# A per-role adapter with layernorm on one Trainium2 core: where the role list is loaded, who spreads it, and the order of TensorE's first work

## The reference

```python
def _L0_cond_ref(role, hidden_states, W_down, b_down, W_up, b_up, gamma, beta):
    h = jnp.einsum('bsh,bhk->bsk', hidden_states, W_down[role]) + b_down[role][:, None, :]
    h = jax.nn.gelu(h, approximate=False)
    u = jnp.einsum('bsk,bkh->bsh', h, W_up[role]) + b_up[role][:, None, :]
    y = hidden_states + u
    mean = jnp.mean(y, axis=-1, keepdims=True)
    var = jnp.mean(jnp.square(y - mean), axis=-1, keepdims=True)
    yn = (y - mean) * jax.lax.rsqrt(var + LN_EPS)
    return yn * gamma[role][:, None, :] + beta[role][:, None, :]
```

## Time and profile before

| | us |
|---|---|
| median of 3 runs | 1421.34 |
| lowest and highest | 1421.17, 1422.79 |
| the profiled execution, its own time | 1421.44 |
| its span in the profile | 1419.7 |
| PE busy | 1405.4 (99%) |
| DVE busy | 1205.7 (85%) |
| ACT busy | 776.7 (55%) |
| POOL busy | 206.7 (15%) |

### The profile page before, as it was taken

The page is one execution under the profiler, slowest core; times in us unless marked ns, Lnnn a source line. Parts: engine busy times, 40 slices in busy tenths (PEclk is TensorE's granted clock), DMA queues, the critical chain, the costliest instruction groups (busy, mean ns, idle before and its releaser), DMA issues.

```text
span 1419.7 us, 29422 instructions
## 1 busy us (share of the span) xinstructions
PE 1405.4 (99%) x6194; PEld 1162.6 (82%) x6195; DVE 1205.7 (85%) x1462; ACT 776.7 (55%) x2048; POOL 206.7 (15%) x310
## 2 busy tenths in 40 slices
PE   8999999999999999999999999999999999999997
PEld 6888888888888888888888888888888888888886
DVE  7798988888888888888899888888888888888887
ACT  5555555555555555555555555555555555555554
POOL 5276311100000000000477310000000000000000
PEclk9999999999999999999999999999999999999999
DMA  7588777766666666666778766776665666566564
GB/s 227 164 234 233 217 202 213 203 200 199 192 185 195 200 189 185 200 199 185 215 228 246 210 204 195 193 221 194 197 195 183 196 200 189 185 195 202 186 188 147
DMA packets 209127, 283.62 MB, mean 200 GB/s; under 512 B 25894, under 2 KB 155814, under 8 KB 209104
## 3 DMA queue, kind: packets, MB, share of 16 engines
q1 hardware_dynamic: 201448, 269.40, 61.3%
q0 software_dynamic: 5984, 12.11, 4.9%
q10 hardware_dynamic: 1672, 1.86, 0.4%
HBM read 183.39 MB, written 99.88 MB: 200 GB/s over the span
## 4 chain that ended last, share of the span: by engine, by line
PE 96%; DVE 1%; issue 1%; DMA 1%; ACTq 0%; DVEq 0%; ACT 0%
PE p_up L1161 16%; PE p_up L1163 16%; PE p_up L1162 16%; PE p_down L1163 16%; PE p_down L1162 16%; PE p_down L1161 16%; DMA row<-in_L_cond_W_down 0%; DMA w_raw<-in_itok_B 0%; ACTq L275 0%; DVE row L909 0%; PE p_down L1204 0%; PE p_down L1209 0%; DVE row L884 0%; PE p_down L1215 0%; DVE row L931 0%
## 5 line engine op out<-in xcount | busy, mean ns | idle before, releaser
L1161 PE MATMUL p_up<-wu_hi,hT_hi 128*128 x1008 | 392.4, 389 | 0.3 <-DVE hT_lo L870 0.3
L1163 PE MATMUL p_up<-wu_hi,hT_lo 128*128 x1008 | 392.2, 389 | 0.0
L1162 PE MATMUL p_up<-wu_lo,hT_hi 128*128 x1008 | 392.1, 389 | 0.0
L1163 PE MATMUL p_down<-wd_hi,xT_lo 128*128 x1000 | 389.0, 389 | 0.0
L1161 PE MATMUL p_down<-wd_hi,xT_hi 128*128 x1000 | 389.0, 389 | 0.0
L1162 PE MATMUL p_down<-wd_lo,xT_hi 128*128 x1000 | 389.0, 389 | 0.0
L643 ACT ACTIVATE hT_hi<-p_hT 128x512 fp32r<-128x512 f32 x126 | 75.5, 599 | 383.0 <-DVE p_hT L864 380.5
L884 DVE SCALAR_TENSOR_TENSOR row<-p_up,row 128x1024 f32<-128x1024 f32 x126 | 154.2, 1223 | 126.1 <-PE p_up L1163 126.0
L623 ACT ACTIVATE xT_hi<-xT_raw 128x1024 fp32r<-128x1024 f32 x125 | 132.7, 1062 | 185.5 <-PE p_down L1163 184.0
L1161 PEld LDWEIGHTS p_up<-wu_hi,hT_hi 128*128 128x128 f32 x1008 | 189.1, 188 | 39.9 <-issue 0.7
L1163 PEld LDWEIGHTS p_up<-wu_hi,hT_lo 128*128 128x128 f32 x1008 | 189.3, 188 | 39.3
(11 more groups left out here) (192 smaller groups left out, 1008.5 us busy)
## 6 DMA issues: line engine op xcount, KB each, us to landing
x_quad<-in_x SPq DMA_DIRECT2D x508, 128.0 KB, 3.4
row<-in_x SPq DMA_DIRECT2D x126, 512.0 KB, 4.1
out<-row SPq DMA_DIRECT2D x126, 512.0 KB, 2.7
h_dram<-h SPq DMA_DIRECT2D x125, 256.0 KB, 4.1
h_quad<-h_dram SPq DMA_DIRECT2D x498, 64.0 KB, 1.9
w_raw<-in_L_cond_W_down POOLq DMA_DIRECT2D x64, 64.0 KB, 3.2
w_raw<-in_L_cond_W_up POOLq DMA_DIRECT2D x64, 64.0 KB, 3.6
row<-in_L_cond_W_up SPq DMA_DIRECT2D x16, 128.0 KB, 5.3
```

The costliest lines, as they stand in the source:

```text
L1161: pe.matmul(dst, a_hi, w_hi, start=first, stop=False)
L1162: pe.matmul(dst, a_hi, w_lo, start=False, stop=False)
L1163: return pe.matmul(dst, a_lo, w_hi, start=False, stop=last)
```

## The change

- The list of roles goes to one partition. The sort keys are made in that partition alone, in other scratch (`key` moves to `w_raw[1]`).
- PE spreads the first role to all partitions with a matmul against a row of ones (`ones_row`, made by POOL with one more memset) after 5 fillers; 21 fillers follow. DVE's `pick_rows` waits for it and copies it out of PSUM first.
- The three spreads of beta and b_down stand ahead of the first matmul of batch 0, and those of b_up a little earlier. ACT's copies wait for the new counts.
- PE loads the slots behind batch 0, whose weights are now at the fixed address 0, and then, ahead of batch 1, spreads the keys with two small matmuls: the row of keys to all partitions, and each key to its own partition. `sort_all` reads both from PSUM, and POOL waits for `key_spread` before it reuses `w_raw`.

```diff
-            sp.dma_start(role_row, role.partition_broadcast(P)).then_inc(roles_loaded, 16)
+            sp.dma_start(role_row, role.rearrange("(o b) -> o b", o=1)).then_inc(roles_loaded, 16)
...
+            pool.memset(ones_row, 1.0).then_inc(iotas_ready, 1)
...
-            pool.wait_ge(half_down, 1)
+            pool.wait_ge(key_spread, 1)
...
-            copy_param(2, p_up[1][:, :], BETA, H, beta_loaded)
+            copy_param(1, p_up[1][:, :], BETA, H, beta_loaded)
...
-            copy_param(1, p_hT[:, :], BD, K, bias_loaded)
+            copy_param(2, p_hT[:, :], BD, K, bias_loaded)
...
             def pick_rows():
-                chain(dve.tensor_scalar(pick_at[:, :], one(FIRST_ROLE), float(-NH), row_of_col[:, 1:2], ALU.mult, ALU.add))
+                dve.wait_ge(role_spread, 1)
+                chain(dve.tensor_copy(role_col[:, :], p_up[1][:, 0:1]))
+                chain(dve.tensor_scalar(pick_at[:, :], role_col[:, :], float(-NH), row_of_col[:, 1:2], ALU.mult, ALU.add))
...
             def sort_all():
                 dve.tensor_scalar(ident, index_row, number_col[:, :], None, ALU.is_equal).then_inc(ident_ready, 1)
-                dve.wait_ge(ident_ready, 3)
-                chain(dve.scalar_tensor_tensor(onehot, key, 1.0, ident, ALU.mult, ALU.mult, accum_out=key_col[:, :]))
-                chain(dve.tensor_scalar(onehot, key, key_col[:, :], None, ALU.is_gt, ALU.add, accum_out=rank[:, :]))
+                dve.wait_ge(key_spread, 1)
+                chain(dve.tensor_copy(key_col[:, :], p_up[1][:, 512 + B:512 + B + 1]))
+                chain(dve.tensor_scalar(onehot, p_up[1][:, 512:512 + B], key_col[:, :], None, ALU.is_gt, ALU.add, accum_out=rank[:, :]))
...
             pe.wait_ge(filler_ready, 1)
-            keep_clock(18)
-            pe.wait_ge(first_known, 2)
-            pe.load(weights_reg, first_slots[0:1, 0:RING])
-            slots = [pe.snap(reg, min_val=0, max_val=1) for reg in weights_reg[0:3]]
-            keep_clock(10)
+            keep_clock(5)
+            pe.wait_ge(role_known, 1)
+            pe.matmul(p_up[1][:, 0:1], ones_row, counts[0:1, FIRST_ROLE:FIRST_ROLE + 1], start=True, stop=True).then_inc(
+                role_spread, 1)
+            keep_clock(21)
...
             def first_product():
-                at = weights_at[0]
-                args = 0, 0, p_down[:, :], at
+                args = 0, 0, p_down[:, :], 0
+                pe.wait_ge(ident_ready, 2)
+                pe.wait_ge(param_rows_split, 1)
+                spread(p_up[1][:, 0:512], 1)
+                spread(p_up[1][:, 512:H], 2).then_inc(params_spread, 1)
+                spread(p_hT[:, :], 0).then_inc(params_spread, 1)
                 pe.wait_ge(half_hi, 1)
                 pe.wait_ge(first_hi, 1)
                 hi_by_hi(*args, range(0, 2))
-                pe.wait_ge(ident_ready, 2)
-                pe.wait_ge(param_rows_split, 1)
-                spread(p_hT[:, :], 0).then_inc(params_spread, 1)
-                spread(p_up[1][:, 0:512], 1)
-                spread(p_up[1][:, 512:H], 2).then_inc(params_spread, 1)
...
-            pe.wait_ge(pieces_split, when_split[0])
             first_product().then_inc(half_down, 1)
             second_product().then_inc(down_done, 1)
+            pe.wait_ge(first_known, 2)
+            pe.load(weights_reg, first_slots[0:1, 0:RING])
+            slots = [pe.snap(reg, min_val=0, max_val=1) for reg in weights_reg[0:3]]
...
+            pe.wait_ge(half_hi, 2)
+            pe.matmul(p_up[1][:, 512:512 + B], ones_row, key, start=True, stop=True)
+            pe.matmul(p_up[1][:, 512 + B:512 + B + 1], key, ones_row[:, 0:1], start=True, stop=True).then_inc(key_spread, 1)
```

More of the change, by code:

```diff
@@ L95, in adapter_kernel @@
         pick_at = sb("pick_at", [P, 1])
+        role_col = sb("role_col", [P, 1])
         spare = sb("spare", [P, SPARE])
@@ L123, in adapter_kernel @@
         table = sb("table", [1, NUMBER + B + 8], I32)
-        index_row, ident, onehot, key = h_quad[:, 0, :].bitcast(I32), *(h_quad[:, n, :] for n in range(1, 4))
+        index_row, ident, onehot = h_quad[:, 0, :].bitcast(I32), h_quad[:, 1, :], h_quad[:, 2, :]
+        ones_row = table[0:1, NUMBER:NUMBER + B].bitcast(F32)
         first_keys = sb("first_keys", [1, 8], I32)
@@ L130, in adapter_kernel @@
          COUNTS) = range(27)
[L131 to L135, removed]
+        counts = sb("counts", [1, COUNTS])
+        role_row, down_row = (w_raw[0][0:1, n * B:n * B + B].bitcast(I32) for n in (2, 3))
+        slot, is_first, is_one, key = (w_raw[1][0:1, n * B:n * B + B] for n in range(4))
+        past_gate, past_mid, step_of = is_first, is_one, w_raw[0][0:1, 3 * B:4 * B]
         rows_raw, rows = h[0:PAIRED, 0:512], wu_hi[0:PAIRED, KC * H:KC * H + 512]
@@ L144, in adapter_kernel @@
         roles_loaded, iotas_ready = sem("roles_loaded"), sem("iotas_ready")
-        sort_step, counted, key_ready, filler_ready = sem("sort_step"), sem("counted"), sem("key_ready"), sem("filler_ready")
+        sort_step, counted, key_ready, key_spread = sem("sort_step"), sem("counted"), sem("key_ready"), sem("key_spread")
         first_known, order_ready, order_in_psum = sem("first_known"), sem("order_ready"), sem("order_in_psum")
@@ L149, in adapter_kernel @@
         chunk_split, role_known, more_rows_loaded = sem("chunk_split"), sem("role_known"), sem("more_rows_loaded")
+        filler_ready, role_spread = sem("filler_ready"), sem("role_spread")
         ident_ready, params_spread, params_landed = sem("ident_ready"), sem("params_spread"), sem("params_landed")
@@ L772, in _ @@
             dve.memset(h[:, 0:512], 0.0).then_inc(param_rows_clear, 1)
-            dve.wait_ge(iotas_ready, 5)
+            dve.wait_ge(iotas_ready, 6)
             dve.tensor_copy(number_col[:, :], index_col[:, :]).then_inc(sort_step, 1)
@@ L779, in _ @@
             dve.wait_ge(roles_loaded, 16)
-            chain(dve.tensor_copy(one(FIRST_ROLE), role_row[:, 0:1]))
+            dve.tensor_copy(one(FIRST_ROLE), role_row[:, 0:1]).then_inc(role_known, 1)
+            dve.wait_ge(role_known, 1)
             dve.tensor_scalar(one(WRAP), one(FIRST_ROLE), 1.0, float(-R), ALU.is_ge, ALU.mult).then_inc(role_known, 1)
@@ L784, in _ @@
             steps[0] += 1
-            dve.wait_ge(role_known, 1)
+            dve.wait_ge(role_known, 2)
             dve.tensor_scalar(one(ONE_ROLE), one(WRAP), float(R - 1), one(FIRST_ROLE), ALU.add, ALU.add).then_inc(role_known, 1)
-            dve.wait_ge(role_known, 2)
+            dve.wait_ge(role_known, 3)
             dve.tensor_scalar(is_one, role_row, one(ONE_ROLE), None, ALU.is_equal, ALU.add,
@@ L800, in _ @@
             dve.wait_ge(key_ready, 1)
-            chain(dve.max(first_keys[:, :], key[0:1, :]))
+            chain(dve.max(first_keys[:, :], key))
             dve.tensor_scalar(first_numbers[:, :], first_keys[:, :], P - 1, P - 1, ALU.bitwise_and,
@@ L807, in pick_rows @@
             def pick_rows():
-                chain(dve.tensor_scalar(pick_at[:, :], one(FIRST_ROLE), float(-NH), row_of_col[:, 1:2], ALU.mult, ALU.add))
-                dve.tensor_scalar(selector[:, 0:1], row_of_col[0:PAIRED, 1:2], counts[0:PAIRED, FIRST_ROLE:FIRST_ROLE + 1], None,
+                dve.wait_ge(role_spread, 1)
+                chain(dve.tensor_copy(role_col[:, :], p_up[1][:, 0:1]))
+                chain(dve.tensor_scalar(pick_at[:, :], role_col[:, :], float(-NH), row_of_col[:, 1:2], ALU.mult, ALU.add))
+                dve.tensor_scalar(selector[:, 0:1], row_of_col[0:PAIRED, 1:2], role_col[0:PAIRED, :], None,
                                   ALU.is_equal).then_inc(ident_ready, 1)
@@ L1240, in first_product @@
                 spread(p_sq[:, 512:H], 4).then_inc(params_spread, 1)
+                spread(p_up[0][:, 0:512], 5)
+                spread(p_up[0][:, 512:H], 6).then_inc(params_spread, 1)
                 pe.wait_ge(first_split, 1)
@@ L1245, in first_product @@
                 lo_by_hi(*args, range(2, 4))
-                spread(p_up[0][:, 0:512], 5)
-                spread(p_up[0][:, 512:H], 6).then_inc(params_spread, 1)
                 spread(p_down[:, :], 0, False)
@@ L1254, in second_product @@
             def second_product():
-                at = weights_at[0]
-                args = 0, 1, p_down[:, :], at
+                args = 0, 1, p_down[:, :], 0
                 pe.wait_ge(x_hi_ready, 1)
@@ L1268, in second_product @@
                 return hi_by_lo(*args, range(6, 8))
+            other = p_up[1][:, 0:K]
+            first_product().then_inc(half_down, 1)
+            second_product().then_inc(down_done, 1)
+            pe.wait_ge(first_known, 2)
+            pe.load(weights_reg, first_slots[0:1, 0:RING])
+            slots = [pe.snap(reg, min_val=0, max_val=1) for reg in weights_reg[0:3]]
             weights_at = [n * (HC * K) for n in slots]
             when_split = [n * (DN + UN) + 1 for n in slots]
-            other = p_up[1][:, 0:K]
-            pe.wait_ge(pieces_split, when_split[0])
```

(5 more changed lines are left out.)

## The result

The changed kernel's median is 1425.13 us (22 executions, 1421.07 to 1426.47), that of the kernel before 1422.34 (22 executions, 1420.88 to 1423.20): a ratio of 1.0015, interval 1.0008 to 1.0021. The forecast was 1420.7 with a range of 1419.2 to 1422.1, so it missed, and on the wrong side. The executions of the changed kernel fall into two groups: 8 of 22 between 1421.07 and 1422.85, 14 between 1424.58 and 1426.47, none in the 1.7 us between. Each execution's mean granted clock goes with them: 0.997 to 0.999 in the lower 8, 0.994 to 0.996 in the upper 14. The kernel before has one group. The profiled execution of the changed kernel is of the upper one (span 1423.4).

The account below looks back on a forecast made before the run. The prediction took the bound to be the moment PE enters its unbroken run, set by loads up to chunk four. Chunk four's -1.4 us plus 0.8 us of added work gave -0.6, from 1421.34 to 1420.7 us, range 1419.2 to 1422.1.

Parts of the forecast that it names:

- What bounds the kernel: Whole run: PE is busy without a break behind the head, so only when it gets into that run counts.
- The load of the roles: Head: one-partition load lands near 2.5 to 3.0 us; role read 1.8 us earlier, down weights issued at 3.9.
- Chunk four earlier by 1.4 us, landing at 16.5: Head: the fourth chunk of down weights lands 1.4 us earlier, bounds 1.05 and 1.8, and is rounded at 17.6.
- 1.8, 0.75 and 0.35: Chunk four's landing: 1.8 us earlier issue, less 0.75 for sharing with x and parameter rows, 0.35 given back.
- Fillers and spreads quick: PE's head: unbroken fillers to about 8.0 us make five slow matmuls quick, saving 1.2 us, costed at nothing.
- PE ready near 15.5 to 16, waiting 1 to 2 us: Ahead of chunk four: PE's earlier gains only lengthen its wait for the chunk, so they count as nothing.
- The clock rival: PE's wait for chunk four drops it to the lower clock; ten matmuls cost 2.4 us, total 1423.1; chance 0.06.
- The added work, 0.8 us: Between batch 0 and batch 1: slots' load and two key matmuls add 0.8 us, bounds 0.4 and 1.3.

Follow-up runs that it names:

- before_again: The kernel before, with register values that waits compare with clamped at zero, profiled a second time; one execution, 1422.15 us.
- late_x2: Changed kernel, clamped, with SP issuing x of batch 2 and the up weights behind it only once chunk four has landed; 1419.54 us, ratio 0.9981 to the kernel before.
- after_clamped: Changed kernel with only the register values that waits compare with clamped at zero; 1425.18 us, ratio 1.0015 to the kernel before.
- keys_in_wait: Changed kernel, clamped, with the slots' load and the keys' two spreads moved from behind batch 0 into PE's wait for chunk four; 1422.10 us, ratio 0.9998.
- fill_wait: Changed kernel, clamped, plus ten unused 512-column matmuls where PE waits for chunk four; 1422.02 us, ratio 0.9999 to the kernel before.
- sp_all: Changed kernel, clamped, with all four quarters of chunk four issued by SP ahead of x of batch 2, none by ACT; 1420.21 us, ratio 0.9990.
- role_wide: Changed kernel, clamped, with the roles loaded to 128 partitions again, everything else reading partition 0; 1425.62 us, ratio 1.0020 to the kernel before.
- role_late: Changed kernel, clamped, narrow load kept, but SP and ACT read the first role only once DVE's keys are ready; 1422.65 us, ratio 1.0001.

## Why the prediction was wrong

Two steps failed. Chunk four did not land where I put it, and PE's longer wait for it, which I costed at nothing, cost it the higher clock in 14 of 22 executions. The second decides the sign: the medians of the two groups are 1425.65 and 1421.85 us, 3.8 apart, and the lower one lies 0.5 under the kernel before.

**What bounds the kernel**: right. The run behind the head is a copy, without waits; only the head changed. From the sorting matmul to the end of the span it is 1393.25 us before and 1392.79 after, and 0.3 of the difference is the wait for a rest of h that only the profile of before has the earlier trace rows.

**The load of the roles**: right. It lands by 2.4 us, the down weights are issued at 3.93 (3.9 forecast). The fixed cost of about 2.0 us that the Trainium skill gives ("DMA: Bandwidth & Descriptors", the anatomy of one DMA) is not met by either shape: 3.90 us wide, under 1.6 us narrow. That section is on DMAs issued by GpSimd, and this load is SP's, so the prediction's comparison was a loose one.

**Chunk four earlier by 1.4 us, landing at 16.5**: the step that failed first. It landed at 17.84. Two things in it were wrong. The starting point, a landing at 17.86, came from one execution, and a quick one: its time lay 0.9 us under the later median, which three runs had not shown, and `before_again` has 19.16. And I let the chunk land "when the bytes ahead of it are through", with 315 GB/s for what it shares. `late_x2` holds back only loads that SP issues beside and behind the last quarter, and that quarter takes 5.03 us instead of 7.44. The difference of 1.4 us is near 19.16 to 17.84 (or 17.09, `after_clamped`), but partly by luck: between those first two profiles the last quarter was issued 2.0 us earlier (12.44 to 10.40) and took 0.7 us longer, and the prediction had 1.8, 0.75 and 0.35.

**Fillers and spreads quick**: right in the profile of the changed kernel (0.71 us for two spreads at 8.92), not always. In `keys_in_wait` the spreads came slow (1.19 us for two) after 2.08 us without work. The head is the same up to there; the fillers ended at 6.86 us in the one and at 7.58 in the other.

**PE ready near 15.5 to 16, waiting 1 to 2 us**: it was ready at 15.28 and waited 3.7. I called PE's gains before the chunk "nothing, since PE then only waits longer". This is the step that failed in the sum. As time ahead of the chunk they are nothing; but the longer wait lost the clock, 3.3 us between two profiles.

**The clock rival**: the mechanism came as described, with the chance wrong by a factor of ten (0.06; 14 of 22 executions) and the price low (2.4 us forecast for ten matmuls; 3.3 between the profiles of `fill_wait` and the changed kernel, which take in the last of batch 0, the keys and half of batch 1). `fill_wait` shows it. The Trainium skill ("TensorE: Matmul & The Clock Gate", why this matters for kernels) warns of idle gaps between bursts, and the trace agrees: 3.68 us idle, then PEclk 0.50. Against it I had set that the wait would be half as long as the 3.38 us ahead of the fillers; it was 3.7 us, and 2.0 us were enough in the profile of `sp_all`. The gaps of up to 0.6 us that "did nothing" could not speak to it, and the earlier trace rows has no wait of PE between 0.3 and 1.2 us.

**The added work, 0.8 us**: right, 0.83 measured in `fill_wait`. -1.4 + 0.8 = -0.6 is also about what the lower group shows: its 8 executions have a median of 1421.85, 0.5 under the median of before. And with x of batch 2 held back in both kernels the difference is 1419.54 - 1420.23 = -0.7 us, or -0.4 when each is taken against the kernel before of its own set (-2.80 and -2.38); that is not clear of the intervals.

**Open**: why the changed kernel moves 222 GB/s between 14 and 17.5 us, and the kernel before 318 and 275. More is in flight at once when the issues come earlier, but `role_wide`, with issues as late as before, has 249. No run here separates the cause. Nor is it shown what decides, in one kernel, whether an execution keeps its clock: that the two groups of the changed kernel differ in it is shown by their mean granted clocks, why they do is not.

## What to carry to other kernels

Work taken off an engine ahead of a load that does not move is not free even where the sum says zero: it becomes idle time, and behind idle time TensorE may run at the lower clock (3.3 us here). Weigh how long the wait will be in a usual execution, and put necessary work (or fillers) into it rather than ahead of it. A load on the path is moved by what is in flight beside it as well as by its own issue: one line that holds back a later, unhurried load gave 2.4 us on the old kernel and 5.6 on the new, where it also kept the clock. One profile is one draw: before an absolute time out of it goes into a sum, see where its execution lies among the others.

## What was not expected of the hardware

- 512 bytes of roles to one partition were read 1.6 us after the issue, the same list to 128 partitions (64 KB) 3.9 to 4.0 us after it.
- The granted clock fell to 0.50 after waits of 3.7 us and, in `after_clamped`, only some 1.7 us after PE had taken up work again. It fell for a shorter stretch after a wait of 1.7 us (`keys_in_wait`), and not after one of 1.3 us (the profiles of `late_x2` and `role_late`).
- Ten matmuls that compute nothing shortened a kernel by 3.2 us, with the load that it waits for no earlier (rounded at 17.95 us, 17.86 without them).
